# A product of a constant ahead of each distance's first product and each group of scores

## The reference

```python
L = where(tri_s, (w @ w.T) * beta, 0) + eye(T)              # w, k, q, v: projections of the sample
A = solve_triangular(L, where(tri_s, w @ k.T, 0), lower=True, unit_diagonal=True)
S = q @ k.T - tril(q @ w.T) @ (beta[..., None] * A)
logits = S * scale + (G[:, None] - G[None, :])              # G: running sum of the gates g
P = softmax(where(tri, logits, -1e30)); o = P @ v           # then @ Wo, times a gate, plus x
```

## Time and profile before

| | us |
|---|---|
| median of three runs | 2256.86 (2245.25 to 2257.46) |
| the profiled execution | 2251.27 |
| its span, first to last instruction | 2249.5 |
| TensorE busy in it | 1976.5 (88%) |
| DVE, POOL, ACT busy | 1624.6 (72%), 925.0 (41%), 866.7 (39%) |
| mean granted clock of TensorE | 0.928 |

### The profile page before, as it was taken

The page is one execution under the profiler, slowest core; times in us unless marked ns, Lnnn a source line. Parts: engine busy times, 40 slices in busy tenths (PEclk is TensorE's granted clock), DMA queues, the critical chain, the costliest instruction groups (busy, mean ns, idle before and its releaser), DMA issues. The chain is left out here.

```text
span 2249.5 us, 43858 instructions
## 1 busy us (share of the span) xinstructions
PE 1976.5 (88%) x16447; PEld 1324.3 (59%) x16455; DVE 1624.6 (72%) x3595; ACT 866.7 (39%) x1694; POOL 925.0 (41%) x917
## 2 busy tenths in 40 slices
PE   4898997998898898898899799989899997778886
PEld 2573563564565465466456357667899996334443
DVE  6969769749948948957966983532367766999995
ACT  2031332233234134234123222223356654777784
POOL 2523413632541551541451353130566664554452
PEclk7998999999999899989989989999999999889998
DMA  3000000000000000000000000312422223010000
GB/s 113 11 1 15 2 2 16 9 14 15 4 20 15 1 21 17 1 21 7 10 17 6 16 8 15 105 35 107 168 72 72 70 74 93 19 38 24 5 12 17
DMA packets 70179, 72.47 MB, mean 32 GB/s; under 512 B 12977, under 2 KB 58593, under 8 KB 69841
## 3 DMA queue, kind: packets, MB, share of 16 engines
q1 hardware_dynamic: 61296, 51.75, 7.7%
q0 software_dynamic: 8672, 17.91, 2.3%
HBM read 38.05 MB, written 27.43 MB: 29 GB/s over the span
## 5 line engine op out<-in xcount | busy, mean ns | idle before, releaser
L669 ACT ACTIVATE a_prep<-ps 128x1536 f32<-128x1536 f32 (+1 forms) x112 | 155.6, 1390 | 332.2 <-PE ps L1304 217.1
L897 DVE TENSOR_REDUCE a_mpart<-ps 128x4 f32<-128x512 f32 (+1 forms) x320 | 190.8, 655 | 46.8 <-PE ps L1245 33.5
L1839 ACT ACTIVATE b_hid<-ps,b_stage 128x128 f32<-128x128 f32 x572 | 163.6, 368 | 139.2 <-PE ps L1954 139.2
L476 POOL TENSOR_TENSOR a_K<-a_K,a_yU 128x480 f32<-128x480 f32 (+14 forms) x120 | 83.5, 696 | 315.3 <-DVE a_yU L842 314.2
L1824 POOL DMA_INDIRECT rows_y<-b_orow,b_target x143 | 164.0, 1147 | 119.4 <-DVE b_orow L1929 116.6
L482 POOL TENSOR_TENSOR a_X<-a_X,a_txy 128x480 f32<-128x480 f32 (+14 forms) x240 | 181.5, 772 | 61.4 <-DVE a_txy L847 59.9
L1117 PE MATMUL ps<-a_txy,cst 128*128 128x480 f32 (+14 forms) x480 | 175.7, 471 | 13.4 <-DVE a_txy L829 12.7
L1954 PE MATMUL ps<-b_hTp,b_stage 128*128 128x128 f32 x1144 | 152.8, 277 | 0.0
L1963 PE MATMUL ps<-b_stage,b_hid 128*128 128x128 f32 x1144 | 151.7, 276 | 0.3 <-ACT b_hid L1839 0.3
L864 DVE TENSOR_TENSOR a_mats<-ps,cst 128x512 f32<-128x512 f32 x112 | 69.9, 684 | 109.8 <-PE ps L1146 109.8
L1559 POOL DMA_INDIRECT rows_h<-a_mats,r_slot x112 | 111.1, 992 | 74.8 <-DVE a_mpart L897 51.2
(11 more groups left out here) (466 smaller groups left out, 4609.8 us busy)
## 6 DMA issues: line engine op xcount, KB each, us to landing
b_hrow<-rows_h SPq DMA_DIRECT2D x143, 65.0 KB, 1.8
b_w<-in_wexp SPq DMA_DIRECT2D x16, 514.0 KB, 9.9
d_got<-rows_y SPq DMA_DIRECT2D x32, 256.0 KB, 3.8
rows_h<-a_txy SPq DMA_DIRECT2D x19, 325.0 KB, 3.1
rows_y<-b_orow,b_target POOLq DMA_INDIRECT x143, 2.4
out<-xs SPq DMA_DIRECT2D x8, 256.0 KB, 2.3
cst<-in_const SPq DMA_DIRECT2D x1, 1865.5 KB, 15.2
rows_h<-a_mats,r_slot POOLq DMA_INDIRECT x112
```

The source lines that it names most:

```text
L669: nc.scalar.activation(Pt[:, at:at + width, :], ps[:, 4:4 + width, :], ACT.Exp).then_inc(e_exp.sem, width)
L897: nc.vector.tensor_reduce(mpart[:, i, j, 4 * g:4 * g + 4], ps[:, 4 + n % 4, :].rearrange("p (r j) -> p r j", r=4)[:, :, 0:128 if i != j el ...
L1839: last = nc.scalar.activation(hid[:, p % 2, f, :], ps[:, p % 2, 128 * f:128 * f + 128], ACT.Gelu, bias=stage[:, p % 3, AT_B1 + f:AT_B1 + f ...
```

## The change

At two places a product of the identity (`identb`, 128 x 128 bf16) with itself four times over (`ident4b`, 128 x 512 bf16) is issued. Nothing reads what it writes, and what follows writes over it.

- In `front`, where it runs beside a `back`, for the distances 2 to 15: into bank 0, ahead of U. It takes over U's wait for `yU` of the distance before (the last reader of bank 0) and, in two of the distances at most, the wait for the routing's use of the bank; U keeps them, and its wait for `tU`. It is a step of its own, so each of the two order strings has 14 more letters f, and each new f stands directly ahead of the f of the U that it belongs to; otherwise the strings are as before.
- In `scores`, for each of the 14 groups of all eight samples: into bank 4, ahead of the first L1295 and behind its wait.

```diff
--- before.py
+++ after.py
@@ -161,9 +161,9 @@
 ORDER_FIRST = ('fffffffffffffffffffffffwfwffwwwwfwfwffwwwwfwfwffwwwwfwfwffwwwwfwfwffwwwwfwfwfwwfwwfwfwffwwwwfwfwffww'
            'wwfwfwffwwwwfwfwffwwwffffwwwffffwwfffwwwwwwwfwwwwwwwwwwwwfwwwwwwwwwwwwfwwwwwwwwwf')
 ORDER_BEGIN = {
-    'pe': ('bbbbbbbbbfbbbbfbfbfbbbfffbbbbbbbbbbfbbbbbfffbbbbbbbbffbbbfbbbfbbbbfffbbbbbbffbbbbbffbbbbbrbbbbbfbbbb'
-           'bfbfbbbbfbbbbfbffbbffbbbbbbbbbfbbbfbbbfbfbfbbfbbbfbfbbbfffbbfbfbbbfbffbfffbbbbbbbffbffbbbbbbbbbfffbb'
-           'bbbbbfffbbbbfbfbbfbbbbbbbfffbbbbbbbfffbbbbbbbfffbbbbbbbfbbbbbbbfbbbbbbbbbfbbbbbbbfbfbb'),
+    'pe': ('bbbbbbbbbfbbbbfbfbfbbbfffbbbbbbbbbbfbbbbbfffbbbbbbbbffbbbfbbbffbbbbfffbbbbbbfffbbbbbffbbbbbrbbbbbffb'
+           'bbbbfbfbbbbfbbbbffbffbbfffbbbbbbbbbfbbbfbbbfbffbfbbfbbbfbffbbbfffbbffbfbbbfbfffbfffbbbbbbbfffbffbbbb'
+           'bbbbbffffbbbbbbbffffbbbbfbfbbffbbbbbbbfffbbbbbbbffffbbbbbbbfffbbbbbbbfbbbbbbbfbbbbbbbbbfbbbbbbbfbfbb'),
     've': ('fbbfbfbbbbfffffffbbfbffffbfbfffffffffffbbbbffffbbbbffffbbbbffffbbbbfrfrbbbbffbrbbbffbbbbffbbbbffbbbb'
            'ffbbbbfbfbfbbbfbfbffffffbbfbbbbbbbbfbbbbbbffbfbfbbbbffbfffbffffffffffffffffffbfffbfffffffffffbffffff'
            'fffffffffffffffbffffffffffffffbbbbbbfffbbbfffbb'),
@@ -171,9 +171,10 @@
     'po': ('bbbbbbbfffffffffffffffbfffbfbbbfbbfbbfffffffffffffffffffffffffff'),
 }
 ORDER_ROUTE = {
-    'pe': ('bbbbbbbbbfbbbbfbfbfbbbfffbbbbbbbbbbfbbbbbfffbbbbbbbbffbbbfbbbfbbbbfffbbbbbbffbbbbbffbbbbbrbbbbbfbbbb'
-           'bfbfbbbbfbbbbrfbffbbfrfbbbbbbbbbfbbbfbbbfbfbfbbfbbbfbfbbbfffbbfbfbbbfrbrffbfffbbbrbbbbffbffbbbbbbbbb'
-           'fffbbbbbbbfffbbbbfbfbbfbbbbbbbfffbbbbbbbfffbbbbbbbfffbbbbbbbfbbbbbbbfbbbbbbbbbfbbbbbbbfbfbb'),
+    'pe': ('bbbbbbbbbfbbbbfbfbfbbbfffbbbbbbbbbbfbbbbbfffbbbbbbbbffbbbfbbbffbbbbfffbbbbbbfffbbbbbffbbbbbrbbbbbffb'
+           'bbbbfbfbbbbfbbbbrffbffbbfrffbbbbbbbbbfbbbfbbbfbffbfbbfbbbfbffbbbfffbbffbfbbbfrbrfffbfffbbbrbbbbfffbf'
+           'fbbbbbbbbbffffbbbbbbbffffbbbbfbfbbffbbbbbbbfffbbbbbbbffffbbbbbbbfffbbbbbbbfbbbbbbbfbbbbbbbbbfbbbbbbb'
+           'fbfbb'),
     'act': ('brrbffbbfbbfffbfbfffffbbbffbfffbfbbbbbbbbbbrrrrbbbbrbrbbbbbbbbfbfbbbb'),
     've': ('frbrbfbfbbbbfffffffbbfbffffbfbfffffffffffbbbbffffbbbbffffbbbbfffrfbbbbffbbbbffbbbbffbbbbffbbbbffbbbb'
            'ffbbbbfbfbfbbbfbfbfffrfffbbfbbbbbbbbfbbbbbbffbfbfbbbbffrbfffbrffrfffrfrfrrfrfrfrfffffrrfrfrfrrrrrrbf'
@@ -1100,6 +1101,12 @@
                         ("X", 10, 0): V.turned(), ("X", 11, 1): V.part()} if routing else {("U", 4): V.begun()}
                 for d in range(1, C):
                     n = NC * (C - d)
+                    if over_back and d >= 2:
+                        yield
+                        pe.wait_ge(*e_yU(d - 2))
+                        if ("U", d) in held:
+                            pe.wait_ge(*held["U", d])
+                        mm(ps[:, 0, :], identb[:, :], ident4b, start=True, stop=True, skip_group_check=True)
                     yield
                     pe.wait_ge(*e_tU(d - 1))
                     if d >= 2:
@@ -1291,6 +1298,8 @@
                             pe.wait_ge(*e_exp(GROUPS[k - 1][-1]))
                         elif lane == 0:
                             pe.wait_ge(*e_mulv())
+                        if lane == 0:
+                            mm(ps[:, 4, :], identb[:, :], ident4b, start=True, stop=True, skip_group_check=True)
                         some = slice(32 * g, 32 * g + (32 if i == j else 24))
                         mm(ps[:, 4 + lane, :].rearrange("p (r i) -> p r i", r=4), aux_l[some, 128 * j:128 * j + 128],
                            aux_m[some, :, 128 * i:128 * i + 128], start=True, stop=False, skip_group_check=True)
```

## The result

The changed kernel takes 2277.98 us (median of four, 2271.05 to 2289.73) against 2255.32 (four, 2245.25 to 2257.46): 1.0115 of the time before, 95% interval 1.0062 to 1.0168. It was measured again beside some of the experiments. The expectation names two theories of the loss, P and W, which stand under The experiments.

What follows compares the result with a forecast made beforehand. TensorE was taken to bound distances 9 to 15 and the scores, DVE distances 1 to 8. Products cost 10.6 + 24.3 = 34.9 us, the clock returns 16.7, leaving 18.2: 2272 us, range 2234 to 2296.

Steps and rivals of the forecast that it cites:

- P: Theory after the result: each product ahead of the scores costs 0.32 us; the clock returns half of its low time.
- W: Theory after the result: each product ahead of the scores costs 0.217 us; the clock returns less than half.
- What bounds: Distances 1 to 8 (64.3 us) are paced by DVE's queue, distances 9 to 15 and the scores (75.9 us) by TensorE.
- The price of one product: Each added product of 512 columns costs 0.217 us, read from four in a row at L1141; 0.44 at half clock.
- its 4.6: First stretch of scores, already at clock 1.00: longer by the whole 21 x 0.217 = 4.6 us.
- Distances 2 to 8 at nothing: 49 products ahead of these distances cost nothing, hidden by TensorE's waits and DVE; upper end 10.6 us.
- What the clock gives back: In the eight stretches of scores a third of 50.0 us returns, 16.7; ends -8.3 and 50.0.
- rival A: The clock holds in the scores; over 70% of low time goes, making the kernel faster, 2233 us; chance 0.25.
- its one half: In the scores each microsecond at half clock loses half: 8.3 us expected, 9.5 measured between first and other stretches.
- lower end below nothing: Clock's return in the scores could be -8.3 us, if the clock also falls in the first sample.

Runs made afterwards that it cites:

- the repeat: The unaltered changed kernel measured and traced once more, against the kernel before: 1.010 (1.007 to 1.013).

## Why the prediction was right, point by point

**What bounds: right.** The scores are TensorE's and the distances 1 to 8 DVE's: the earlier trace rows and the stretches above.

**The price of one product: right for U, too small for S.** U: 0.23 us by the rows, 0.217 forecast; 0.42 at half clock. S: 0.29 on the mean instead of 0.217, because the forecast read it from L1141, four equal products in a row. It had no term for the step from 128 rows to a row group, nor for what stands ahead of S. The first sample, at full clock in both, lost 4.0 us to 13 S and 8 U (the forecast's 14 and 7 are off by one each), 0.6 less than its 4.6: there some of the price goes into waits. With groups alone the first stretch took 69.7 us at 1.00, which is 3.3 / 13 = 0.25 for each S.

**Distances 2 to 8 at nothing: right as a cost there, wrong as an account.** Their stretches shrank by 3.5 us in all. What was missed is what these 49 products do for the scores: 1.0119 without them against 0.9962 with them on the same chip (0.9996 with them on another). The forecast had put their worth at nothing and the clock's return on the products in the scores. The low time in the stretches of scores says that neither kind does it alone: 100 us before, 86 with U alone and 100 with S alone (both on the slower chip), 25 and 49 with both (the change and its repeat), and 13 with all U and two of the 14 groups. The U's of all distances and S at groups 9 and 10 hold the clock; the other 12 S pay their price for little.

Why each has its place can be read from where the clock fell in the kernel before. In the stretch from 1130.9 us on it fell at 1134.4, 1148.0 and 1178.7. The five microseconds ahead of each:

```profile
1129.40:1134.40 5.00, 3.24 (x50) 1.83 (x49) 4.93 (x17) 1.45 (x1) 2.58 (x4) 1.00 0.00 0
...
1143.00:1148.00 5.00, 4.88 (x42) 2.64 (x43) 4.80 (x17) 0.00 (x0) 1.89 (x3) 1.00 0.00 0
...
1173.70:1178.70 5.00, 4.97 (x72) 3.27 (x73) 1.28 (x5) 1.61 (x2) 3.62 (x7) 1.00 0.12 40
```

The first fall comes behind waits of TensorE, that of 1.05 us ahead of distance 8 the longest, where the last near U stands; the third, 47.8 us in, lies between the scores of groups 9 and 10. With U alone the first is gone and a late one of 10.2 us is left, 49.0 us in. The prediction read the earlier trace rows as falls of a busy engine; that holds for the third, not for the first.

**What the clock gives back: more of it came than taken.** Low time in the stretches of scores was 100.1 us by the earlier trace rows. After, it is 6 x 0.02 x 2 x 76.1 = 18.3 and 0.05 x 2 x 63.0 = 6.3, together 24.6. So 75% went in this execution, not a third, past the 70% at which rival A was to decide. In the repeat it was 49.2 us, so 51% went. A didn't come, for three reasons. The price was higher. The clock fell in other places (below). And low time is not lost by half. Two stretches of one trace with the same products, all U and groups 8 to 11, show that; three others of it read 72.3 us at 1.00.

```profile
1125.60:1199.40 73.80, 69.62 (x907) 44.10 (x906) 42.92 (x134) 22.51 (x20) 38.02 (x51) 0.98 0.05 16
1304.30:1381.20 76.90, 73.90 (x907) 46.19 (x906) 42.73 (x134) 22.50 (x20) 34.73 (x51) 0.91 0.05 16
```

At 0.91 it is 13.8 us low and 76.9 - 72.3 = 4.6 us longer: 0.33 for each low microsecond, not 0.5. With groups alone the same step (82.0 us at 0.92, 92.1 at 0.78) gives 0.37. Part of the rest turns into waits of TensorE. The waits in the stretch with two groups, then before (who for whom, us in total, times, longest):

```profile
PE ps L1116 <- DVE a_tU L824: 1.9, 2, 1.1
...
PE ps L1124 <- DVE a_txy L830: 0.5, 1, 0.5
```

```profile
PE ps L1109 <- DVE a_tU L823: 1.0, 1, 1.0
```

So of the 75.5 us of low time that went, 25 to 28 came back (an estimate, at 0.33 to 0.37). With the 12.2 by which the scores grew, their products cost 37 to 40 us. The forecast had 16.7 and 34.9. The check that the prediction used for its one half (9.5 us for a clock of 0.89 against 1.00) compared the first sample with others that have the routing's work in them.

**Missed altogether: falls where no product was added**, 8.2 us between the samples and 4.7 ahead of the last sample's scores. Between the samples TensorE waits 2.2 us for DVE ahead of L1075 (L1074 before), in both kernels; before, the clock stayed up. What makes it fall there now isn't shown. The forecast looked for the clock's return where the products stand and had no term for a fall elsewhere, not even in its "lower end below nothing". With two groups only one of the six such stretches in the profile is longer, 42.7 us; the others read 40.6 or 40.7, as before.

So the right direction came from the right mechanism: products paid for in TensorE's own stretch, and a clock that returns less than they cost. That 18 stands near the measured 24.6 of the profile is partly luck. In the scores, where the whole forecast lay, 18.2 was forecast and 12.2 measured (21.6 in the repeat). The other 12.4 came from places for which it had no term.

The rule of the Trainium skill (TensorE: Matmul & The Clock Gate, "Why this matters for your kernels") ties the return to half clock to idle gaps. The first fall above does come behind waits. The other two come from an engine busy for 4.88 and 4.97 of 5 us, and in the repeat's first stretch of scores the clock fell with none at all ahead of it:

```profile
245.70:250.70 5.00, 5.00 (x47) 2.37 (x47) 4.73 (x11) 0.00 (x0) 2.21 (x4) 1.00 0.00 0
250.70:254.10 3.40, 3.40 (x13) 1.60 (x9) 0.00 (x0) 1.45 (x1) 0.00 (x0) 0.50 0.02 5
```

So gaps alone do not account for the falls in this kernel, and neither does TensorE's busy share. By the rule, S gives nothing back, since it stands where there is no gap. Judged by its time (1.0167), S alone did give next to nothing back; beside U it gave more.

## What to carry to other kernels

In this kernel a product issued only for the clock paid where it was dense and stood in TensorE's waits, shortly ahead of the stretch that TensorE bounds. Inside that stretch nearly every one is paid, and more where it forces a new step from 128 rows to a row group. Count the falls of the clock one by one, place a product against each, and look again afterwards for falls that moved. Profile more than one execution: the low time in the scores differed by a factor of two between two of the same kernel. The best versions found here (all U, groups 8 to 11 or 9 and 10) came to 0.9996, 0.9962 and 0.9976: a gain of 0 to 0.4%, too small to be sure of.

## What the runs showed of the hardware that was not expected

A product of 16 columns in the same places cost 2.9%, more than one of 512 (1.1%). In the runs with groups alone, of 16 columns, on 32 rows and without the near distances some stretches of scores had a mean clock of 0.75 or 0.78 and took 89.6 to 92.1 us. Most of their low time is one long piece, here without the near distances:

```profile
1368.40:1373.40 5.00, 5.00 (x76) 3.33 (x68) 2.97 (x11) 1.87 (x2) 3.99 (x6) 1.00 0.10 30
1373.40:1407.40 34.00, 34.00 (x268) 19.76 (x256) 4.85 (x20) 8.84 (x7) 13.94 (x21) 0.50 0.08 25
```

TensorE worked for all of these 34 us and the clock stayed at half. What begins and ends such a piece is open.

On the chip where the kernel before took 2287 us, ACT and DVE waited in most samples for something that no engine's instruction released, here with the near distances alone ahead of an exponential, with TensorE waiting behind it:

```profile
1197.73 1.45 ACT L670 ACTIVATE a_prep<-ps 128x1536 f32<-128x1536 f32 x1 [3.99 <-remote]
...
1199.24 0.39 PE L1303 MATMUL ps<-a_aux_g,a_aux_l 32*128 32x512 bf16 x3 [1.69 <-ACT a_prep L670]
```

These waits (with all distances alone 18.7 us in five of ACT's L670 and 52.1 in six of DVE's L855) are in no trace of the other chips. What they wait for wasn't tried.
